# Talking-heads attention: the mixing products cut into 64 by 64 pieces

## What is computed

```python
q = split_heads(x @ wq.T + bq)
k = split_heads(x @ wk.T + bk)
v = split_heads(x @ wv.T + bv)
attn = jnp.einsum('bhnd,bhmd->bhnm', q, k) * scale
attn = jnp.einsum('gh,bhnm->bgnm', th1_w, attn) + th1_b[None, :, None, None]
attn = jax.nn.softmax(attn, axis=-1)
attn = jnp.einsum('gh,bhnm->bgnm', th2_w, attn) + th2_b[None, :, None, None]
out = jnp.einsum('bhnm,bhmd->bhnd', attn, v)
out = out.transpose(0, 2, 1, 3).reshape(B, N, D)
return out @ wo.T + bo
```

## Time and profile before

| | |
|---|---|
| time, median of 3 runs | 4690.89 us (4690.49 to 4691.51) |
| profiled execution: span | 4688.7 us |
| mean granted TensorE clock | 0.991 |
| TensorE products and weight loads | 58206 each |
| talking heads, first to last mixing product | 1337.9 to 3963.3 us of the span |

### The profile page before, as it was taken

How to read it: one execution, slowest core, us unless ns; L and a number is a source line. 1 busy time by engine, 2 the same in 40 slices (tenths; PEclk the granted TensorE clock), 3 DMA queues, 4 the chain that set the end, 5 groups by cost and what they waited for, 6 DMA issues and landing times. The chain is left out here.

```text
span 4688.7 us, 141401 instructions
## 1 busy us (share of the span) xinstructions
PE 4554.5 (97%) x58206; PEld 3744.1 (80%) x58206; DVE 2549.3 (54%) x7440; ACT 2183.1 (47%) x5035; POOL 1671.0 (36%) x2777
## 2 busy tenths in 40 slices
PE   6999998999889999999999999999999999999998
PEld 4666665776678888888888888888888888899998
DVE  5667886666555555455555555555555544442333
ACT  3443443555545554554455455445545544212443
POOL 1103335777633333333333333333333333001555
PEclk8999999999999999999999999999999999999999
DMA  4112110000000000000000000000000000232333
GB/s 109 23 30 48 38 31 7 1 2 1 1 14 2 13 13 2 20 13 13 3 13 13 2 13 13 7 8 13 13 2 13 13 3 17 74 90 66 65 65 56
DMA packets 122476, 110.77 MB, mean 24 GB/s; under 512 B 63975, under 2 KB 110396, under 8 KB 121844
## 3 DMA queue, kind: packets, MB, share of 16 engines
q1 hardware_dynamic: 94447, 66.34, 6.1%
q0 software_dynamic: 16768, 23.59, 2.9%
q10 hardware_dynamic: 10628, 11.80, 1.1%
HBM read 59.76 MB, written 41.48 MB: 22 GB/s over the span
## 5 line engine op out<-in xcount | busy, mean ns | idle before, releaser
L1937 POOL TENSOR_TENSOR th_qg<-th_qT,w_th_th 128x180 f32<-128x180 f32 x1760 | 846.3, 503 | 1617.1 <-PE PS L2231 1607.5
L2231 PE MATMUL PS<-th_kT,th_qg 64*125 64x274 f32 x10560 | 1420.5, 400 | 0.0
L2130 ACT ACTIVATE th_P<-PS 110x600 f32<-110x600 f32 x880 | 647.0, 735 | 1119.1 <-PE PS L2218 1119.1
L2048 DVE TENSOR_REDUCE th_nmx<-PS 125x1 f32<-125x548 f32 x880 | 641.0, 728 | 902.8 <-PE PS L2231 902.8
L2218 PEld LDWEIGHTS PS<-th_mixn,th_P 61*110 61x110 f32 x17600 | 985.8, 173 | 96.0 <-issue 20.2
L2231 PEld LDWEIGHTS PS<-th_kT,th_qg 64*125 64x125 f32 x10560 | 947.5, 184 | 136.9 <-issue 0.2
L2218 PE MATMUL PS<-th_mixn,th_P 61*110 61x60 f32 x17600 | 980.2, 254 | 3.5 <-ACT th_P L2130 1.8
L2140 ACT ACTIVATE th_P<-PS,th_nb 125x548 f32<-125x548 f32 x880 | 621.0, 706 | 106.9 <-DVE th_nb L2051 106.9
L1370 POOL TENSOR_SCALAR ga_P<-ga_P,ga_rw 110x110 f32<-110x110 f32 (+4 forms) x240 | 264.9, 1115 | 160.3 <-DVE ga_rw L1538 159.5
L2051 DVE TENSOR_SCALAR th_nb<-th_nmx,w_th_b 125x1 f32<-125x1 f32 x880 | 240.1, 273 | 32.2
L2256 PEld LDWEIGHTS PS<-th_P,th_v 110*32 110x32 f32 x11520 | 229.7, 110 | 28.6 <-issue 27.5
(11 more groups left out here) (364 smaller groups left out, 6407.3 us busy)
## 6 DMA issues: line engine op xcount, KB each, us to landing
pf_xT<-pf_spill SPq DMA_DIRECT2D x32, 412.5 KB, 5.4
ex_tokens<-th_xn SPq DMA_DIRECT2D x124, 82.5 KB
pf_spill<-pf_xT SPq DMA_DIRECT2D x16, 412.5 KB, 3.7
ex_turned<-th_rT SPq DMA_DIRECT2D x16, 412.5 KB, 3.1
ex_x<-ex_turned SPq DMA_DIRECT2D x32, 206.2 KB, 4.4
out_h<-X SPq DMA_DIRECT2D x16, 330.0 KB
ex_w<-in_L_ffn_W ACTq DMA_DIRECT2D x18, 288.0 KB
ex_w<-in_L_ffn_W ACTq DMA_DIRECT2D x8, 576.0 KB
```

Source lines behind the costliest of these rows:

```text
L1937: ins = pool.tensor_tensor(qg[:, m % SB, :, 64 * s:64 * s + HQ].rearrange("p c (h n) -> p c h n", n=QH), qT[:, im % 2, :, at + s * QH:at + ...
L2048: dve.tensor_reduce(nmx[:, p:p + 1], PS[0:MR, bank:bank + 2, 0:HK], AX.XY, ALU.max, negate=True) \
L2130: act.activation(P2[:, :, :, at * QT:(at + 1) * QT].rearrange("p t h (s n) -> p s (t h) n", s=2), PS[0:R, MB:MB + 2, 0:VO].rearrange("p s ...
L2231: ins = pe.matmul(PS[0:MR, bank + a, 0:HK], qg[s, p, c, 0:MR], kT[s, im % 2, c, :], start=c == 0, stop=c == NC - 1)
```

## The change

The 548 keys are now counted in two halves of 274, and each half in five pieces of KP = 55 (the last piece of a half ends in a padding column). A group of keys is therefore 55 keys of the first half, on partitions 0 to 54, and 55 of the second, on partitions 64 to 118, with nine unused partitions between; PK = 119.

- Mixing: each product by 110 keys becomes two by 55 keys, one to PSUM partitions 0 to 54 and one to 64 to 118, so there are four pieces of 61 rows by 55 columns per group of keys: two row halves by two column halves. There are 20 products a tile.
- Scores are unchanged.
- `P` gets a padding column after each half of the keys; the exponential writes to two halves.
- `v` has the same layout of keys: the value projection has 64 tokens stationary, twice, on the column halves (20 products a sample). `xT` gets eight more columns, zeroed by POOL, since the last window reads past the end.
- The values product contracts 119 partitions in place of 110, and ACT's copy takes 119 partitions.
- At the start of the stage DVE zeroes the unused PSUM partitions (two instructions, before its first step); TensorE waits for them before the first mixing, and its warming products go to another bank.

```diff
+HK = N // 2
+KP = NP // 2 // T
+PK = 64 + KP
+XW = NP + 8
-        v = sb("v", [R, 2, T, H, 32])
+        v = sb("v", [128, 2, T, H, 32])
-        P = sb("P", [MR, SB, NP])
-        P2 = sb("P2", [R, T, H, QL * QT])
+        P = sb("P", [MR, SB, 2, HK + 1])
+        P2 = sb("P2", [PK, T, H, QL * QT])
...
+                for q in (32, 96):
+                    dve.memset(PS[q:q + 32, MB:MB + 2, 0:VO], 0.0).then_inc(gapped, 1)
...
-                                       PS[0:R, MB:MB + 2, 0:VO].rearrange("p s (x n) -> p s x n", n=QH), ACT.Copy).then_inc(p2_in, 1)
+                                       PS[0:PK, MB:MB + 2, 0:VO].rearrange("p s (x n) -> p s x n", n=QH), ACT.Copy).then_inc(p2_in, 1)
...
-                            to = PS[0:R, bank + t // 2 if t < 4 else bank + 1, t % 2 * D:(t % 2 + 1) * D]
+                            o, at = bank + t // 2 if t < 4 else bank + 1, t % 2 * D
                             for c in range(KC):
-                                ins = pe.matmul(to, xT[0:kin(c), c, t * R:(t + 1) * R], wv[0:kin(c), c, :],
-                                                start=c == 0, stop=c == KC - 1)
+                                for a in range(2):
+                                    n0 = a * HK + t * KP
+                                    ins = pe.matmul(PS[a * PC:(a + 1) * PC, o, at:at + D], xT[0:kin(c), c, n0:n0 + PC], wv[0:kin(c), c, :],
+                                                    start=c == 0, stop=c == KC - 1)
...
                         for t in range(T):
-                            for s in range(2):
-                                a = slice(64 * s, 64 * s + HQ + 1)
-                                ins = pe.matmul(PS[0:R, MB + s, t * HQ:(t + 1) * HQ], P[a, p, t * R:(t + 1) * R], mixn[a, p],
-                                                start=True, stop=True)
+                            for a in range(2):
+                                for s in range(2):
+                                    q = slice(64 * s, 64 * s + HQ + 1)
+                                    ins = pe.matmul(PS[64 * a:64 * a + KP, MB + s, t * HQ:(t + 1) * HQ], P[q, p, a, t * KP:(t + 1) * KP],
+                                                    mixn[q, p], start=True, stop=True)
...
-                                                    v[:, b % 2, t].rearrange("p h d -> p (h d)")[:, at:at + 32], P2[:, t, h, 0:nq],
+                                                    v[0:PK, b % 2, t].rearrange("p h d -> p (h d)")[:, at:at + 32], P2[:, t, h, 0:nq],
```

More of the change, by code:

```diff
@@ L1794, in talking_heads @@
     nc, X, PS, ident = k.nc, k.X, k.PS, k.ident
-    HALF, HK = NP // 2, N // 2
+    HALF = NP // 2
     NT = B * NTILE
@@ L1812, in talking_heads @@
         xn = sb("xn", [R, T, D])
-        xT = sb("xT", [C + 1, KC, NP])
+        xT = sb("xT", [C + 1, KC, XW])
         rT = sb("rT", [C + 1, KC, NP])
@@ L1828, in sem @@
             return nc.alloc_semaphore("th_" + name)
-        ready = sem("ready")
+        ready, gapped = sem("ready"), sem("gapped")
         var, powed, xn_in = sem("var"), sem("powed"), sem("xn_in")
@@ L1918, in _ @@
             def _(pool):
-                pool.memset(xT[C:C + 1], 1.0).then_inc(ready, 1)
+                pool.memset(xT[C:C + 1, :, 0:NP], 1.0).then_inc(ready, 1)
                 pool.wait_ge(ready, 1)
@@ L1923, in _ @@
                 pool.wait_ge(powed, 1)
-                for i, (a, x) in enumerate(((rT[C:C + 1], 1.0), (qg[:], 0.0), (P[:], 0.0), (v[:], 0.0))):
+                for i, (a, x) in enumerate(((rT[C:C + 1], 1.0), (qg[:], 0.0), (P[:], 0.0), (v[:], 0.0), (xT[:, :, NP:XW], 0.0))):
                     pool.memset(a, x).then_inc(ready, 1)
@@ L2103, in take @@
                             ins = act.activation(v[:, im % 2, 0:4, :, 0:HD].rearrange("p (a t) h d -> p a (t h) d", a=2),
-                                                 PS[0:R, bank:bank + 2, 0:2 * D].rearrange("p a (t d) -> p a t d", d=HD), ACT.Copy)
+                                                 PS[:, bank:bank + 2, 0:2 * D].rearrange("p a (t d) -> p a t d", d=HD), ACT.Copy)
                         else:
-                            ins = act.activation(v[:, im % 2, 4, :, 0:HD], PS[0:R, bank + 1, 0:D].rearrange("p (h d) -> p h d", d=HD),
+                            ins = act.activation(v[:, im % 2, 4, :, 0:HD], PS[:, bank + 1, 0:D].rearrange("p (h d) -> p h d", d=HD),
                                                  ACT.Copy)
@@ L2139, in _ @@
                             act.wait_ge(mixed, m - SB + 1)
-                        act.activation(P[:, p, 0:N].rearrange("p (a n) -> p a n", a=2), PS[0:MR, bank:bank + 2, 0:HK], ACT.Exp,
+                        act.activation(P[:, p, :, 0:HK], PS[0:MR, bank:bank + 2, 0:HK], ACT.Exp,
                                        bias=nb[:, p:p + 1], accum_out=rs[:, p:p + 1]).then_inc(prob, 1)
@@ L2187, in product @@
                     elif part[0] == "V":
+                        if im == 0:
+                            pe.wait_ge(ready, 6)
                         for t in range(4) if part == "V03" else (4,):
-                            to = PS[0:R, bank + t // 2 if t < 4 else bank + 1, t % 2 * D:(t % 2 + 1) * D]
+                            o, at = bank + t // 2 if t < 4 else bank + 1, t % 2 * D
                             for c in range(KC):
-                                ins = pe.matmul(to, xT[0:kin(c), c, t * R:(t + 1) * R], wv[0:kin(c), c, :],
-                                                start=c == 0, stop=c == KC - 1)
+                                for a in range(2):
+                                    n0 = a * HK + t * KP
+                                    ins = pe.matmul(PS[a * PC:(a + 1) * PC, o, at:at + D], xT[0:kin(c), c, n0:n0 + PC], wv[0:kin(c), c, :],
+                                                    start=c == 0, stop=c == KC - 1)
                     else:
@@ L2200, in product, with stream @@
                     ins.then_inc(done[part[0]], 1)
-                def stream(count):
+                def stream(count, bank=MB):
                     for _ in range(count):
-                        pe.matmul(PS[:, MB, 0:2 * D], ident[0:C, :], wk[0:C].rearrange("p c n -> p (c n)"), start=True, stop=True)
+                        pe.matmul(PS[:, bank, 0:2 * D], ident[0:C, :], wk[0:C].rearrange("p c n -> p (c n)"), start=True, stop=True)
                 TAIL = {"Y03": 4, "Ra": 7, "La": 1}
-                stream(5)
+                stream(5, 2 * SB - 1)
                 pe.wait_ge(ready, 1)
@@ L2214, in _ @@
                             pe.wait_ge(p2_in, n)
+                        else:
+                            pe.wait_ge(gapped, 2)
                         for t in range(T):
-                            for s in range(2):
-                                a = slice(64 * s, 64 * s + HQ + 1)
-                                ins = pe.matmul(PS[0:R, MB + s, t * HQ:(t + 1) * HQ], P[a, p, t * R:(t + 1) * R], mixn[a, p],
-                                                start=True, stop=True)
+                            for a in range(2):
[3 more added lines that the diff above has]
+                                                    mixn[q, p], start=True, stop=True)
                         ins.then_inc(mixed, 1)
```

## The result

The changed kernel takes 4576.8 us (median of four runs, 4573.4 to 4578.6) against 4691.0 for the kernel before beside it (4690.5 to 4691.5): a ratio of 0.9758, with a 95% interval of 0.9744 to 0.9772. That is 114 us less; 132 were forecast, and the time lies within the range.

What follows compares the result with a forecast made beforehand. TensorE was taken to set the pace, with mixing bound by its loads. Savings of 85 us (709 ordinary tiles) and 51 (171 behind items) made 136, less 2.4 and 1.4: 132 us off, 4559 us; range 4535 to 4640 us.

Steps and rivals of the forecast that it cites:

- What bounds the kernel: TensorE sets the pace in the score and mixing tiles, 2.37 us each; mixing is bound by its loads.
- Part 1, the rounds: Mixing: ten rounds of four 55-column pieces at once, 0.053 us each, where loads followed each other every 0.097.
- rival B: Mixing: instruction issue bounds the rounds at 0.078 us; +88 us, 4779 us; chance 0.06.
- rival A: Mixing: only two pieces run at once, so 20 rounds of 0.053 us; +334 us, 5025 us; chance 0.06.
- rival C: Mixing: weak issue bound or late copy, rounds of 0.06 to 0.065 us; 4620 to 4665 us; chance 0.12.
- Rival E: TensorE: the idle gaps, 0.14 to 0.2 us long, lower the granted clock; chance 0.01.
- Part 2, the gaps: Shape changes around mixing: two gaps with bare loads; tile 2.25 us against 2.37, behind an item 1.93 against 2.23.
- 0.05 + 0.09: From the last mixing round to the scores' first load: 0.05 us, then a 0.09 us gap.
- The sequencer: TensorE's sequencer passes mixing's 80 loads and products in 1.0 us, 12 ns each; 0.7 us ahead, some 0.4 under the load.
- Rival D: Gap from 64 by 64 pieces is shorter, at most 0.04 us once a tile; 4525 us; chance 0.05.
- Part 3: The rest: value projection costs 2.4 us, DVE's two zeroings before the first statistics 1.4 us.
- The value projection's 2.4 us: Group 4's value projection follows the logits with a new gap and bare load: 0.15 x 16 = 2.4 us.

Runs made afterwards that it cites:

- experiment 5: Changed kernel with each mixing product streaming 30 of 60 columns, so half of the mixed heads is left out: 4539.8 us.
- experiment 6: Changed kernel with mixing streaming 30 of 60 columns and loading 40 of 55, leaving work out: 4437.6 us.
- experiment 3: Changed kernel with the key-half loop outside the loop over the five groups, same 20 mixing products in another order: 4879.8 us, ratio 1.0407.
- experiment 4: Changed kernel with the mixing products of each array quarter in a row (key half, then row half, outermost): 5509.5 us.
- experiment 9: Changed kernel with 12 instead of 60 values products in a group, four of five key tiles left out of the values: 4380.2 us.
- experiment 7: Changed kernel with DVE's two zeroings moved from the stage's start to step 12 of the sample ahead of the first: 4575.3 us, ratio 0.9753.
- experiment 1: Changed kernel with the scores cut into quarters too, so scores and mixing use one array shape: 4425.4 us, ratio 0.9427.
- experiment 2: Kernel before with only the scores cut into quarters, mixing left as it was: 4905.1 us, ratio 1.0457.

## Why the prediction was right

**What bounds the kernel** held: TensorE's own sequence of rounds and gaps set the tile, and no other engine came onto the path.

**Part 1, the rounds** (0.053 us forecast) measured 52.5 ns. Experiments 5 and 6 show that it was right for its reason: stream first, load close behind, issue under 38 ns. They rule out rival B. The round itself rules out rival A, and rival C's rounds of 0.06 us and more: four pieces start within 21 ns of one another, and each four 52.5 ns after the four before, 13 ns a pass. Rival E is out too, with a mean granted clock of 0.990 to 0.992 in all four runs. The Trainium skill, TensorEngine Tiling (Array Packing), Performance Considerations, gives each product some 60 cycles of overhead. Paid one after another that would have made 4973 us, an estimate. The trace does not agree, with 13 ns a pass where the estimate takes 25. What can spoil the packing is the order: in experiments 3 and 4, where the four pieces are not neighbours, the kernel is 303 and 933 us slower.

**Part 2, the gaps.** 0.32 us ahead of mixing measured 0.317; the run of mixing from its first load to its last round 0.518 (forecast 0.525); the bare score load and five rounds 1.27 (forecast 1.265). The term that was mis-sized is the gap ahead of the scores, "0.05 + 0.09": counted from the first pass of the last round it is 0.160 us and not 0.14, because the four passes of a round start 7 ns apart and the gap begins at the last of them. The tile became 2.264 and not 2.25, and 0.104 us was saved where the forecast says 0.12 (2.368 less 2.25, rounded up). Behind an item, from mixing's first load to the last score round, 1.943 were measured against 1.93; it was 2.230 before. The counts were 706 and 174 tiles instead of 709 and 171. Together 706 x 0.104 + 174 x 0.287 = 73 + 50 = 123 us, not 136.

**The sequencer** was called "enough, with little over", "the next thing to be late". It was costed at nothing, and this is the second failed term: 18 stalls, 8 us. The wait was for instructions, but not at the pace of 12 ns that the forecast looked at: all 18 stalls stand at the start of a block of 256, 1.3 to 1.6 us after its packet landed. They come where 240 instructions of the values and 80 of the mixing fall within 3.3 us, and go with most of the values (experiment 9); the forecast looked at one mixing's instructions and not at what stood before them. Rival D, a shorter gap from smaller pieces, had something in it only when the load was cut (128 ns in experiment 6), which the change does not do.

**Part 3.** The zeroings hold up the first statistics by 1.2 us and the first mixing by about 1 to 2 us (experiment 7), where 1.4 were forecast. The value projection's 2.4 us did not show: from the first start of each run of logits' products, and of value projection products, to whatever follows it are 32.8 + 57.8 us in sum before and 33.8 + 57.0 after.

**The sum.** From the first mixing pass to the last are 2625.4 us before and 2511.6 after, 113.8 less, against 123 less 8 from the terms above. Ahead of it the changed run has 4.2 us more, of which some 2 lie in the stages before this one, and behind it 2.3 less; so the span is 111.9 less.

## What to carry to other kernels

Cut a product so that load and stream are equally long, but then give its neighbours on TensorE the same cut: a change of shape cost some 0.17 us of idle gap and bare load each time (two to a tile, which went from 2.26 to 1.92 us without them), and the neighbour's equal cut, whose own rounds take no longer, was worth more (151 us) than the change (114). Write the pieces that are to run together next to each other in the order, innermost. Count TensorE's instructions over some microseconds around the shortest ones. A tile at one in 22 ns had hardly a stall outside the bursts of values at 11 ns; with a tile at one in 15 ns and the same bursts there were about a hundred, and 75 us of waits, which the profile only calls issue, stood against a saving of 151.

## What the runs showed of the hardware

**Instructions come in blocks of 256 and can run out.** In the kernel of experiment 1 the packets of the instruction queue are seldom closer than 3.4 us in the stage (first percentile of the times from start to start; the lowest is 3.3, the median 4.1), which is 13.3 ns for each of 256 instructions; in the changed kernel these are 3.6 (lowest 3.3) and 5.1. A tile of experiment 1 has 128 instructions in 1.92 us, 15 ns each, and its values 240 in 2.57, 11 ns each; it stalls about a hundred times inside mixings. A tile of the changed kernel has 104 in 2.26, 22 ns each, and 15 of its 18 stalls are right behind values. The kernel before, with 64 in 2.37, 37 ns each, has 3 beside the two at the stage's end. Every stall at a block's start, in all these kernels, comes 1.2 to 1.9 us after the landing of the block's packet, so it is the packet that comes late. Why packets come no closer together stays open: no run changed the transfers and left the instructions alone.

**About three passes wait at a busy piece** while later instructions for other pieces go ahead (experiments 3 and 4: the next piece starts when three passes of each busy one are still to come). No other order was run.

**The gap at a change of shape** is neither a fixed sum after the stream nor one of row halves alone: 143 ns from the last mixing pass to the scores in the changed kernel, 187 in experiment 2 with 110-column loads ahead of it, 128 with 40-column loads, 34 without a change of shape. From 40 to 55 columns of load it grows by 0.8 ns a column (128 to 140 ns, with 30 columns streamed in both), and from 55 to 110 by 0.8 (143 to 187, with 60 streamed), about the pace of a load.
